# The first batch of a fused linear-attention and expert-choice kernel: its load and layer norm in halves

## The reference, cut to what matters

```
x = L0_attn_x                       # 16 x 1024 x 256, f32
xn = layernorm(x)                   # per token, over 256
Q, K, V = xn @ Wq.T + bq, xn @ Wk.T + bk, xn @ Wv.T + bv
Q, K = elu(Q) + 1, elu(K) + 1       # 16 heads of 16
KV, K_sum = sum over tokens of K (x) V, of K
attn = (Q @ KV) / (Q . K_sum + 1e-6) @ Wo.T + bo
probs = softmax(xn @ gate_w)        # 8 experts; each takes its top 256 of 1024 tokens of a batch
ffn = scatter-add over experts of g * (gelu(xin @ w1[e]) @ w2[e])
out = x + attn + bf16(ffn)
```

## Time and profile before

| | us |
|---|---|
| three runs | 1902.72, 1903.57, 1904.08 (median 1903.57) |
| the profiled execution's own time | 1903.31 |
| its span, first to last instruction | 1901.6 |
| PE busy | 1868.1 (98%) |
| DVE, ACT, POOL busy | 1278.4, 1270.6, 1030.7 |

### The profile page before, as it was taken

One profiled execution on the slowest core, in us unless ns is written; L12 is line 12 of the kernel. 1 busy time (PEld: TensorE's weight loads), 2 busy tenths in 40 slices (PEclk: granted clock), 3 DMA queues, 4 the chain that ended last, 5 costly groups with the idle time before them and its releaser, 6 DMA issues.

```text
span 1901.6 us, 39471 instructions
## 1 busy us (share of the span) xinstructions
PE 1868.1 (98%) x13818; PEld 1275.2 (67%) x13818; DVE 1278.4 (67%) x2579; ACT 1270.6 (67%) x2045; POOL 1030.7 (54%) x947
## 2 busy tenths in 40 slices
PE   6999999999999999999999999999999999999998
PEld 4566666666676666666666666666666666666666
DVE  6677888888757777755787875555555555555556
ACT  6988887767746666666666666666666666666665
POOL 5656566666445554554455555545554555555453
PEclk9999999999999999999999999999999999999999
DMA  6888788879665655665667667576766666676857
GB/s 176 230 221 245 212 252 233 232 231 249 196 184 131 129 120 121 147 178 147 168 151 186 153 160 178 133 183 152 190 154 158 169 140 183 155 187 154 183 120 222
DMA packets 448901, 338.24 MB, mean 178 GB/s; under 512 B 224757, under 2 KB 430330, under 8 KB 448762
## 3 DMA queue, kind: packets, MB, share of 16 engines
q1 hardware_dynamic: 383674, 253.84, 48.1%
q0 software_dynamic: 48864, 66.88, 19.4%
q10 hardware_dynamic: 16224, 15.73, 2.5%
HBM read 185.61 MB, written 100.40 MB: 150 GB/s over the span
## 4 chain that ended last, share of the span: by engine, by line
PE 70%; DMA 1%; DVE 0%; issue 0%; ACT 0%; POOL 0%; SPq 0%; POOLq 0%
PE pY L1951 35%; PE pH L1936 35%; DMA lacc<-acc 1%; DMA acc<-yo,idx 0%; POOL acc L1710 0%; PE pR L295 0%; ACT lffn L1746 0%; DVE yo L1812 0%; PE pN L235 0%; PE pN L279 0%; DVE lmix L1861 0%; DVE fffn L1858 0%; ACT hid L1735 0%; DVE hid L1796 0%; ACT gel L1732 0%
## 5 line engine op out<-in xcount | busy, mean ns | idle before, releaser
L1951 PE MATMUL pY<-w2s,hid 128*128 128x256 f16 x6144 | 756.6, 273 | 0.8 <-DVE hid L1796 0.8
L1936 PE MATMUL pH<-xgT,w1s 128*128 128x512 f16 (+1 forms) x3120 | 747.7, 376 | 1.3 <-PEq L324 1.3
L1951 PEld LDWEIGHTS pY<-w2s,hid 128*128 128x128 f16 x6144 | 599.7, 98 | 180.7 <-DVE yo L1812 3.6
L1710 POOL DMA_INDIRECT acc<-yo,idx x254 | 407.0, 1602 | 521.4 <-DVE yo L1812 448.4
L1796 DVE SCALAR_TENSOR_TENSOR hid<-gel,cur,hid 128x512 f16<-128x512 f32 (+1 forms) x520 | 384.7, 740 | 445.5 <-ACT hid L1735 437.0
L1732 ACT ACTIVATE gel<-pH,cur 128x512 f32<-128x512 f32 (+1 forms) x520 | 353.7, 680 | 476.9 <-PE pH L1936 456.3
L1936 PEld LDWEIGHTS pH<-xgT,w1s 128*128 128x128 f16 x3120 | 305.2, 98 | 252.4 <-DMA xgT<-xg 1.6
L1735 ACT ACTIVATE hid<-gel,cur 128x512 f16<-128x512 f32 (+1 forms) x520 | 372.1, 715 | 16.8
L219 POOL DMA_INDIRECT xg<-table,idx x256 | 286.7, 1120 | 112.1 <-issue 58.2
L1260 PE MATMUL pP<-wkv,xT 128*128 128x512 f16 x768 | 201.7, 381 | 5.8 <-DVE bias_rows L974 4.7
L722 POOL TENSOR_SCALAR xm<-xring,moments 128x256 f32<-128x256 f32 x128 | 128.1, 1010 | 71.1 <-DVE xhl L995 71.0
(11 more groups left out here) (235 smaller groups left out, 1887.6 us busy)
## 6 DMA issues: line engine op xcount, KB each, us to landing
stage<-in_w SPq DMA_DIRECT2D x160, 512.0 KB, 6.4
xring<-in_x SPq DMA_DIRECT2D x16, 1024.0 KB, 6.0
x2ring<-in_x SPq DMA_DIRECT2D x16, 1024.0 KB, 6.9
table<-xhl SPq DMA_DIRECT2D x32, 512.0 KB, 4.0
mix<-x2ring SPq DMA_DIRECT2D x32, 512.0 KB, 3.3
acc<-zeros SPq DMA_DIRECT2D x16, 1024.0 KB, 4.7
fmix<-mix SPq DMA_DIRECT2D x48, 256.0 KB, 2.9
facc<-acc SPq DMA_DIRECT2D x48, 256.0 KB, 3.8
```

The costliest lines, as they stand in the source:

```text
L1710: g.indirect_dma_start(acc, bass.IndirectOffsetOnAxis(ap=idx[q][:, s:s + 1], axis=0), yo[i][:, s, :], None, compute_op=ALU.add).then_inc(a ...
L1936: last = t.matmul(pH[hc % 4][:, tok], w[:, aw, c, hc * P:(hc + 1) * P], xgT[i][:, ad, c, tok], start=k == 0 and c == 0, stop=k == 2 and c ...
L1951: last = t.matmul(pY[s // 2][:, s % 2, :], hid[:, hc % 4, ad, s * P:(s + 1) * P], w[:, aw, hc, :], start=hc == 0 and k == 0 and s % 2 == 0 ...
```

## The change

The load of x of batch 0 is split: its first four tiles come before the weights, its last four after them, with events `x_first` and `x_in`. Each weight has its own semaphore, and the order is Wk, Wv, Wq, gate, Wo. The seven bias DMAs move from SP's queue to ACT's. The statistics, the norm and the root of the first four tiles have their own steps (event `first_norm`); those of the last four come later on DVE, behind the weights' work. ACT runs one Exp on a single column ahead of its wait. PE turns the fourth weight behind the fold of the maxima; its first `project` puts the products with the weights' rests and the bias last, and waits for them only there. In batch 0 alone, `high` and `low` of tiles 4 to 7 come one tile later: at j = 1 to 4 in place of 0 to 3, and ACT's `high` stands behind `keys`. The semaphores of the last stores are merged.

```diff
             def _(sp):
-                sp.dma_start(xring[:, 0, :, :], x_rows[0]).then_inc(x_in, 16)
-                for i, w in ((1, Wk), (2, Wv), (0, Wq), (3, Wo)):
-                    sp.dma_start(wraw[:, i, :, :], ...).then_inc(w_in, 16)
-                sp.dma_start(graw[:, :, :], ...).then_inc(w_in, 16)
-                value = held(sp, at(consts, 0, 0))
-                ...   (seven bias DMAs)
+                sp.dma_start(xring[:, 0, 0:HALF, :], x_rows[0][:, 0:HALF, :]).then_inc(x_first, 16)
+                weight_load(1, Wk)
+                weight_load(2, Wv)
+                weight_load(0, Wq)
+                sp.dma_start(graw[:, :, :], ...).then_inc(g_in, 16)
+                weight_load(3, Wo)
+                sp.dma_start(xring[:, 0, HALF:NT, :], x_rows[0][:, HALF:NT, :]).then_inc(x_in, 16)
                 value = held(sp, at(x_in, 0))
                 sp.wait_ge(consts, 1)
                 sp.wait_ge(x_in, value)
                 sp.dma_start(xring[:, 1, :, :], x_rows[1]).then_inc(x_in, 16)
                 sp.dma_start(x2ring[:, 0, :, :], x_rows[0]).then_inc(x2_in, 16)
 # POOL
-                norm(0)
+                norm_first()
                 for j in range(HALF):
                     centre(0, j)
+                norm(0)
 # ACT
+                act.wait_ge(consts, at(consts, 0, 0))
+                for r in range(2):
+                    act.dma_start(bias_raw[r:r + 1, 0:D], ...).then_inc(b_in, 16)
+                    act.dma_start(bias_raw[r:r + 1, D:2 * D], ...).then_inc(b_in, 16)
+                act.dma_start(bo_row[:, :], ...).then_inc(b_in, 16)
+                for c in range(DC):
+                    act.dma_start(bqT[:, c:c + 1], ...).then_inc(b_in, 16)
                 act.wait_ge(consts, at(consts, 0, 4))
-                act.wait_ge(rstd_done, at(rstd_done, 0))
+                a.activation(gexp[:, 0, 0, 0:1], ident[:, 0:1], ACT.Exp)
+                act.wait_ge(first_norm, at(first_norm, 0, 4))
                 for j in range(HALF):
                     high(0, j)
                 weights_high()
...
-                        if j < HALF:
+                        if n > 0 and j < HALF:
                             high(n, j + HALF)
                         elif nxt and HALF < j < NT - 1:
                             high(n + 1, j - HALF)
                         keys(n, j)
+                        if n == 0 and j == 1:
+                            act.wait_ge(rstd_done, at(rstd_done, 0))
+                        if n == 0 and 1 <= j <= HALF:
+                            high(0, j + HALF - 1)
 # DVE
                 bias_factors()
-                for j in range(NT):
+                for j in range(HALF):
                     stats_of(0, j)
-                moments_of(0)
-                weight_maxima()
-                root_of(0)
+                moments_first()
+                largest_of(2, 1)
+                largest_of(3, 2)
+                root_first()
+                largest_of(0, 0)
+                other_maxima()
                 fold_maxima()
...
                 low(0, 2)
                 low(0, 3)
+                for j in range(HALF, NT):
+                    stats_of(0, j)
+                moments_of(0)
                 weight_rest(3)
                 weight_rest(2)
+                root_of(0)
...
-                        if j < HALF:
+                        if n == 0 and 1 <= j <= HALF:
+                            low(0, j + HALF - 1)
+                        elif n > 0 and j < HALF:
                             low(n, j + HALF)
 # PE
-                pe.wait_ge(w_in, at(w_in, 0, 4))
-                for i, dst in ((1, pP[1]), (2, pQ), (0, pO), (3, pD)):
+                turn_weights(1, pP[1])
+                turn_weights(2, pQ)
+                turn_weights(0, pO)
...
+                turn_weights(3, pD)
...
+                    at_first = n == 0 and j == 0
+                    terms = [(0, 0), (1, 0), (0, 1)] if at_first else [(0, 0), (0, 1), (1, 0)]
+                    if at_first:
+                        pe.wait_ge(whi, at(whi, 0, 1))
                     for k, (a, b) in enumerate(terms):
+                        if at_first and k == 2:
+                            pe.wait_ge(wlow, at(wlow, 0, 1))
+                            pe.wait_ge(lhs_done, at(lhs_done, 0, 2))
+                            pe.wait_ge(bias_step, at(bias_step, 0, 2))
+                            t.matmul(pP[j % 2][:, 0:D], bias_lhs[:, :], bias_rows[:, :], ...)
 # SP, the end
-                for i in range(EP):
-                    sp.wait_ge(lout[i], at(lout[i], 0))
-                for u in range(4):
-                    sp.wait_ge(end_out[u], at(end_out[u], 0))
+                sp.wait_ge(lout, at(lout, 0, EP - 1))
+                sp.wait_ge(end_out, at(end_out, 0, 3))
```

More of the change, by code:

```diff
@@ L436, in qz_of @@
                 return (eq, qraw)[h] if m == NB - 1 else qz[h]
-            w_in = event("w_in", step=16)
+            w_in = [event(f"w_in{i}", step=16) for i in range(4)]
+            g_in = event("g_in", step=16)
             b_in = event("b_in", step=16)
+            x_first = event("x_first", step=16)
+            first_norm = event("first_norm", per=5)
             wmaxed = event("wmaxed")
@@ L504, in block_program, with tiles_of_norm @@
             last_mixed = x2ring[:, (NB - 1) % 2, :, :]
+            def tiles_of_norm(n):
+                return slice(HALF, NT) if n == 0 else slice(0, NT)
             block = ctx.enter_context(nc.Block())
@@ L903, in stats_of @@
                 def stats_of(n, j):
-                    if j == 0:
+                    if n == 0 and j == 0:
+                        dve.wait_ge(x_first, at(x_first, 0))
+                    elif n == 0 and j == HALF or j == 0:
                         dve.wait_ge(x_in, at(x_in, n))
@@ L908, in stats_of @@
                         last.then_inc(stat_done, 1)
+                    if n == 0 and j == HALF - 1:
+                        last.then_inc(first_norm, 1)
                 def moments_of(n):
@@ L920, in moments_of, with moments_first, root_first @@
                     dve.wait_ge(stat_done, value)
-                    for j in range(NT):
+                    for j in range(HALF if n == 0 else 0, NT):
                         last = v.bn_aggr(moments[:, j, :], stats[:, j, :])
                     last.then_inc(aggr_done, 1)
+                def moments_first():
+                    dve.wait_ge(first_norm, at(first_norm, 0, 0))
+                    for j in range(HALF):
+                        last = v.bn_aggr(moments[:, j, :], stats[:, j, :])
+                    last.then_inc(first_norm, 1)
+                def root_first():
+                    dve.wait_ge(first_norm, at(first_norm, 0, 3))
+                    v.tensor_scalar(rstd[:, 0:HALF], rpow[:, 0:HALF], XSCALE, None, ALU.mult).then_inc(first_norm, 1)
                 def bias_factors():
@@ L1261, in project @@
                                             stop=k == 2 and c == DC - 1, skip_group_check=True)
-                            if k == 0 and c == 0:
+                            if k == 0 and c == 0 and not at_first:
                                 t.matmul(pP[j % 2][:, 0:D], bias_lhs[:, :], bias_rows[:, :], start=False, stop=False, skip_group_check=True)
@@ L1494, in block_program @@
             ldone_pool = event("ldone_pool")
-            lout = [event(f"lout{i}", step=16) for i in range(LP)]
+            lout = event("lout", per=LP - 2, step=16)
             EP = LP - 2
@@ L1508, in block_program @@
             end_done = event("end_done", per=4)
-            end_out = [event(f"end_out{u}", step=16) for u in range(4)]
+            end_out = event("end_out", per=4, step=16)
             def end_tiles(u):
```

58 lines of the change are left out of this document (33 added, 25 removed).

## The result

The changed kernel took 1907.76 us (median of 18 runs), the kernel before 1904.16 in the same runs: ratio 1.0019, 95% interval 1.0013 to 1.0026. That is 3.6 us later; I had forecast 1.2 and a range that ends at 1907.0. The profiled execution has a span of 1905.8 us against 1901.6.

The account below looks back on a forecast made before the run. PE, busy 98% of the span, was taken to bound the kernel, with batch 0's shift passing on. Tile 5 0.8 us later plus 0.4 for the clock gave +1.2 us: 1904.8 us, range 1901.8 to 1907.0.

Parts of the forecast that it names:

- The start: PE's first project in batch 0: starts at 17.6 instead of 19.50, 1.9 us earlier, bounds 1.4 to 2.6.
- the transposes of the first tiles are held by the loads: SP's queue: tile 0's transpose, issued near 11.5 behind two loads, lands 1.2 us behind their last byte, at 17.5.
- The low clock at the start: PE's first tiles: low clock may hold up to 0.8 us more work back; 1.5 us gain taken at keys of tile 1.
- The middle: Up to project of tile 5, batch 0: 2.5 us lost against 1.5 to 1.9 gained before, so 0.8 us later.
- two waits end together: Project of tile 5: transpose lands at 34.6, gate's differences come 0.6 us later than before; either alone would hold PE.
- The clock behind the hold: After PE's idle 3.1 us before project of tile 5: a clock fall would cost 1.4 us, a quarter taken, 0.4.
- rival 1: Clock falls during PE's wait before project of tile 5: 0.8 + 1.4, +2.2 us, 1905.8; chance 0.42 forecast's, this one 'clock' 0.24.
- Rival 2: Tile 5's transpose lands after 35.5, clock falls (1.4), later transposes held again (0.5): +3.9 us, 1907.5; chance 0.08.
- Rivals 3: Loads do not hold the transposes; PE starts at 14.3 to 15, gate's differences alone decide: -2.4 us, 1901.2; chance 0.12.
- 4: Start's gain kept whole because the wait at the gate is shorter: -4 to -4.5 us, 1899.3; chance 0.05.
- 5: Wait at tile 5 ends with the same landing as before (33.7), all shifts vanish: 0 us, 1903.6; chance 0.09.
- The merged semaphores at the end: Last stores at the kernel's end: 0, at most 0.3 us gained.

Follow-up runs that it names:

- experiment 4: Changed kernel, but SP issues x of batch 1 and x2ring without waiting for the second half of x of batch 0: 1905.79 us, ratio 1.0005 to the kernel before.
- experiment 1: Changed kernel with high and low of tiles 4 to 7 of batch 0 back in their old order: 1903.32 us against 1904.69 for the kernel before.
- experiment 5: Changed kernel with 12 useless matmuls on PE ahead of its wait in gate of tile 4, batch 0: 1906.58 us, ratio 1.0014 to the kernel before.
- experiment 6: Changed kernel with DVE's low of tile 7 moved behind gate_max in batch 0: 1909.37 us, ratio 1.0023 to the kernel before.
- experiment 7: Changed kernel with the transpose of tile 5 issued ahead of the table store and x of batch 2, in batch 0: 1907.94 us, ratio 1.0016 to before.
- experiment 8: Changed kernel with low of tile 7 behind gate_max and the transpose of tile 5 ahead of store and load: 1906.84 us, ratio 1.0009 to before.
- experiment 2: Kernel before with only high and low of tiles 4 to 7 one tile later in batch 0: 1909.66 us, ratio 1.0024.
- experiment 3: Kernel before with only one single-column Exp ahead of ACT's wait, putting the table load in idle time: 1905.08 us against 1904.69, ratio 0.9999.
- experiment 9: Changed kernel with the old order of tiles 4 to 7 and x of batch 1 and x2ring issued without the wait: 1902.11 us against 1905.14 before.

## Why the prediction was wrong

**The start: the first step that failed, 1.2 us too early.** I had 17.6 for the first project, measured 18.80. SP issued x of batch 1 at 9.46 (I had 9.2). Then I let the two loads run at full rate from 1.0 us behind the issue, because the very first bytes had come that soon. Bytes are not yet flow: the row is at 123 GB/s from 11.2 and at 328 only from 11.6, 2.1 us behind the issue. The row of the kernel before had shown it: its first load was issued at 0.81 and the row reaches 351 GB/s only at 3.2. The x2ring load landed 8.2 us behind its issue at 9.88, at 18.1, where my last byte at 15.7 to 16.3 and 0.7 us to landing gave 16.4 to 17.0. That the transposes of the first tiles are held by the loads was right, and experiment 4 shows it. The Trainium skill, "DMA: Bandwidth & Descriptors" (Queues, rings and completion order), says that each DMA engine takes the descriptors of a ring in their order; the trace agrees: the transpose of tile 0, issued at 10.7 behind both loads, lands at 18.8, 0.7 us behind the second of them.

**The low clock at the start: not settled by one pair of profiles.** I allowed 0.4 for it (a shift of 1.5 left of 1.9, at worst 1.1). In the profile of the changed kernel tiles 0 and 1 took 5.73 us against 4.48, 1.25 more, so that at tile 2 it stood 0.55 us behind, where I had it 1.5 ahead. But that difference is mostly luck of the two profiles. The six profiles with the changed kernel's start (changed and experiments 1, 5, 6, 7 and 8) took 4.48 to 5.73 us, 4.92 in the mean, and the three with the start of before (before and experiments 2 and 3, the last with its one Exp more on ACT) 4.48 to 5.73, 5.01 in the mean. In the mean, tile 2 starts at 23.80 in the six and at 24.45 in the three: 0.65 ahead, where I had 1.5. So no longer low clock is shown for the change; what is shown is that the gain at the first project was 0.7 us and not 1.9.

**The middle: right.** I had 2.3 us lost from there to tile 5 (from 1.5 ahead to 0.8 behind); measured 12.09 - 9.85 = 2.24. That two waits end together was right: gate at 36.38, transpose at 36.6; experiments 6 and 7 take away one each and win nothing in the middle, 8 takes both away and wins 2.0. The times (34.1, 34.6) were off by 2.0 to 2.3, about what the profile stood behind my forecast at tile 2 (2.05).

**The clock behind the hold: the second step that failed.** I had the idle time right (3.1 us; measured 3.25) and the price near (1.4), but took only a quarter of it into the sum, 0.4. The clock fell, as rival 1 had it, and cost 1.63 us here, 1.61 by experiment 5. What I weighed 3.1 against was 1.65 us, which had not been enough, and 3.8, a stretch in which PE was idle; the whole idle time before the first project was 4.70.

**The sum.** In the two profiles: -0.70 + 1.25 + 2.24 + 1.63 = +4.42 us at batch 1, and +3.99 near the end of the stage. With the mean of the starts in place of the two profiles' own: -0.65 + 2.24 + 1.63 = +3.2, against +3.6 in the medians. Against my +1.2 (-1.5 + 2.3 + 0.4) the start accounts for 0.85 and the clock for 1.23. Rival 2 came nearest, at +3.9 with a chance of 0.08: its condition, a landing after 35.5, held (36.6), its fall of the clock (1.4) came, and its 0.5 for later transposes held again did not, since with the clock kept up (experiment 5) nothing is left behind tile 5 (9.63 against 9.61). Rivals 3, 4 and 5 are out.

**Still open.** Between batch 1 and the end of the stage the difference to before changes by -1.7 to +0.8 us from kernel to kernel (experiment 9 gains 1.7 there, experiment 3 loses 0.8). One place of it can be read, PE's wait for ACT's query projections (`qraw`) near 62 to 67 us: 1.65 us before, 0.77 in experiment 9, and 2.08 in experiment 3, where the clock fell behind it and six matmuls took 2.74 us instead of 1.47:

```profile
67.12 2.74 PE L1308 MATMUL pQ<-xT,wq 128*128 128x512 f16 x6 [2.08 <-ACT qraw L817]
```

Single profiles do not tell whether that belongs to a kernel or to an execution. The merged semaphores at the end were not tried alone; the difference is 3.99 us near the end of the first stage and 4.2 in the whole spans, nothing that shows a gain.

## What to carry to other kernels

Work moved ahead brings only what the next wait lets through: here 4.7 us on the compute engines became 0.7, because the load that the next issue waits for was put last and the queue ran dry. Moving one step behind another on an in-order engine moves everything behind it: look for the short step that another engine waits for (here the differences to the maximum, 0.19 us), and for the DMAs issued after it. And where two waits end together, take both away before you judge either. An idle stretch of PE that is long enough for the clock to fall has a second price behind it: here 3.25 us of waiting and then 1.6 us of slow work. And compare a start that depends on the clock over several profiles, not over one pair.

## What the runs showed of the hardware that was not expected

The same two first tiles took 4.48 to 5.89 us in eleven profiles in which PE came from idle, with no relation to the edits that I can see (4.48 and 5.73 in kernels whose start is the same: before and experiment 2, and again experiment 7 and the changed kernel). How long the low clock lasts differs between executions, and up to 1.25 us of a single profile's start is chance. The Trainium skill, "TensorE: Matmul & The Clock Gate" (Part 1), says that the point of the change varies by about half a microsecond from run to run; the spread of the two tiles' time here, 1.4 us, is larger.

The clock also fell behind a shorter wait than the hold: behind 2.08 us of idle time in experiment 3 (67.12), but not behind 1.95 in experiment 8 (38.11).

A DMA queue that had run dry needed 1.7 us from the issue until the row passed 100 GB/s for good (9.46 to 11.2), and 2.1 us until it passed 300. The first load of all is no faster: issued at 0.81, it passes 300 GB/s at 2.8 in the changed kernel.
